# Gate times bias added to x by an accumulating DMA per group, in place of a product per tile on TensorE

## The reference, cut to what matters

```
mod = (silu(c) @ wmod).reshape(8, 6, 1, 512)
sa, ca, ga, sb, cb, gb = ...            # rows of each batch; ga and gb are gates
x = x + ga * attention(...)             # for most rows: x + ga * bo, the same row V for a whole batch
h = layernorm(x) * (1 + cb) + sb
xd = dequantised(quantise(h)); wd = dequantised(quantise(weight))
x = x + gb * (xd @ wd.T + bias)         # = x + xd @ (gb*wd).T + gb*bias
```

## Time and profile before

| | us |
|---|---|
| median of 3 runs (390.23 to 390.87) | 390.24 |
| profiled execution, its own time | 389.05 |
| its span | 387.2 |
| PE busy | 321.5 |
| DVE busy | 306.0 |
| ACT busy | 219.8 |
| POOL busy | 203.9 |
| mean granted TensorE clock | 0.942 |

### The profile page before, as it was taken

How to read it: one execution, slowest core, us unless ns; L and a number is a source line. 1 busy time by engine, 2 the same in 40 slices (tenths; PEclk the granted TensorE clock), 3 DMA queues, 4 the chain that set the end, 5 groups by cost and what they waited for, 6 DMA issues and landing times.

```text
span 387.2 us, 6242 instructions
## 1 busy us (share of the span) xinstructions
PE 321.5 (83%) x2302; PEld 244.5 (63%) x2302; DVE 306.0 (79%) x500; ACT 219.8 (57%) x498; POOL 203.9 (53%) x123
## 2 busy tenths in 40 slices
PE   2940075785999999999899998979999989985994
PEld 0100012574798887788787776868887777664883
DVE  1893497699864699698979787999887899799733
ACT  2001858573835777787594969677876776110310
POOL 2004886909928549554973868294939372600000
PEclk9995569589999999999999999999999999998999
DMA  7998445769945884959394869566955951102032
GB/s 264 387 407 318 95 70 212 124 215 298 200 156 124 260 148 179 186 197 216 112 239 158 203 163 246 137 172 164 268 123 182 210 139 69 42 0 109 25 139 81
DMA packets 23156, 68.10 MB, mean 176 GB/s; under 512 B 2563, under 2 KB 2692, under 8 KB 19022
## 3 DMA queue, kind: packets, MB, share of 16 engines
q1 hardware_dynamic: 14982, 51.67, 37.6%
q0 software_dynamic: 7392, 14.68, 23.9%
q10 hardware_dynamic: 752, 1.36, 1.2%
HBM read 50.50 MB, written 17.20 MB: 175 GB/s over the span
## 4 chain that ended last, share of the span: by engine, by line
PE 43%; DVE 28%; issue 9%; ACT 7%; POOL 6%; DMA 4%; SPq 1%; DVEq 0%; POOLq 0%; ACTq 0%
PE ps L574 8%; PE ps L575 8%; PE ps L579 8%; PE ps L557 4%; DVE DD L1002 3%; DVE XL L965 3%; PE ps L655 3%; DVE amax L984 3%; PE ps L531 2%; DVE WL L972 2%; PE ps L570 2%; DMA v_bc<-mod_scratch 2%; DVE X L1009 2%; POOL U L326 2%; POOL U L328 2%
## 5 line engine op out<-in xcount | busy, mean ns | idle before, releaser
L326 POOL TENSOR_TENSOR U<-U,c_bc 128x1024 f32<-128x1024 f32 x32 | 78.3, 2448 | 54.2 <-ACT U L391 54.2
L574 PE MATMUL ps<-WH,XH 128*128 128x512 f32 x256 | 101.7, 397 | 0.7 <-ACT XH L375 0.7
L575 PE MATMUL ps<-WL,XH 128*128 128x512 f32 x256 | 101.5, 396 | 0.0
L375 ACT ACTIVATE XH<-ps 128x512 fp32r<-128x512 f32 x64 | 37.9, 592 | 81.6 <-PE ps L557 81.5
L328 POOL TENSOR_TENSOR U<-U,sb_bc 128x1024 f32<-128x1024 f32 x32 | 76.8, 2400 | 2.5
L965 DVE TENSOR_TENSOR XL<-ps,XH 128x512 fp32r<-128x512 f32 x64 | 44.0, 687 | 39.8 <-ACT XH L375 39.7
L579 PE MATMUL ps<-WH,XL 128*128 128x512 f32 x256 | 69.7, 395 | 1.3 <-DVE XL L965 1.3
L391 ACT ACTIVATE U<-X,nmr,rstd 128x512 f32<-128x512 f32 x64 | 48.5, 808 | 27.9 <-DVE nmr L980 27.8
L579 PEld LDWEIGHTS ps<-WH,XL 128*128 128x128 f32 x256 | 48.5, 190 | 12.4 <-DVE XL L965 2.0
L575 PEld LDWEIGHTS ps<-WL,XH 128*128 128x128 f32 x256 | 48.8, 191 | 11.1
L402 ACT ACTIVATE unused<-X 128x512 bf16<-128x512 f32 x64 | 39.4, 618 | 28.5 <-POOL X L317 27.6
(11 more groups left out here) (209 smaller groups left out, 404.1 us busy)
## 6 DMA issues: line engine op xcount, KB each, us to landing
X<-in_x SPq DMA_DIRECT2D x16, 1024.0 KB, 4.9
out<-X SPq DMA_DIRECT2D x15, 1024.0 KB, 5.8
X<-mod_scratch POOLq DMA_DIRECT2D x14, 1024.0 KB, 10.1
X<-in_wmod SPq DMA_DIRECT2D x4, 1024.0 KB, 9.6
c_bc<-mod_scratch SPq DMA_DIRECT2D x6, 256.0 KB, 7.7
sb_bc<-mod_scratch SPq DMA_DIRECT2D x6, 256.0 KB, 7.8
Wd<-in_w SPq DMA_DIRECT2D x1, 1024.0 KB, 12.9
U<-in_wmod SPq DMA_DIRECT2D x1, 1024.0 KB, 15.0
```

The costliest lines, as they stand in the source:

```text
L326: nc.gpsimd.tensor_tensor(a, a, spread(c_bc[:, b % 2, :]), ALU.mult).then_inc(u_done, 1)
L574: M(bank, XH[:, n % 2, r], WH[:, b % 2, k, :], start=False, stop=False)
L575: M(bank, XH[:, n % 2, r], WL[:, b % 2, k, :], start=False, stop=False)
```

## The change

The product with G2 goes, and with it G2, its loads, its two rows in DRAM and the split of GBIAS. In their place POOL issues, behind modulate(g), an accumulating DMA of the row GBIAS into X1's slot of group g, of the same form as the one that adds V. `add_tile` waits for it at a group's first tile. Before the first one POOL waits until GBIAS is written to DRAM.

```
-            sp.wait_ge(g2_rows, 2)
-            sp.dma_start(mod_dram[:, GBH, :], XH[0:B, 0, :].bitcast(F32)).then_inc(g2_rows_out, 16)
-            sp.dma_start(mod_dram[:, GBL, :], XL[0:B, 0, :].bitcast(F32)).then_inc(g2_rows_out, 16)
-            sp.wait_ge(g2_rows_out, 32)
-            for b in range(2):
-                load_g2(b)
+            sp.wait_ge(gb_row, 1)
+            sp.dma_start(mod_dram[:, GBIAS, :], mrow[GBIAS]).then_inc(gbias_out, 16)
...
-                if t % 2 == 0 and 2 <= t and t + 2 < GROUPS:
-                    sp.wait_ge(y_done, TILES * t)
-                    load_g2((t + 2) // 2)
...
+            def add_row(g, which):
+                nc.gpsimd.dma_start(X1[:, g % XSLOTS, :, :],
+                                    mod_dram[g // 2:g // 2 + 1, which, :].unsqueeze(1).to_broadcast([P, TILES, D]),
+                                    accum_op=ALU.add).then_inc(x_added[g % XSLOTS], 16)
+
+
+            def add_bias(g):
+                if g == 0:
+                    pool.wait_ge(gbias_out, 16)
+                pool.wait_ge(z_done, TILES * (g + 1))
+                add_row(g, GBIAS)
...
                 modulate(g)
+                add_bias(g)
...
-                M(bank, onesr[:], G2[:, b % 2, :], start=True, stop=False)
                 pe.wait_ge(xh_done, n + 1)
                 for k in range(NC):
                     r = slice(k * P, (k + 1) * P)
-                    M(bank, XH[:, n % 2, r], WH[:, b % 2, k, :], start=False, stop=False)
+                    M(bank, XH[:, n % 2, r], WH[:, b % 2, k, :], start=k == 0, stop=False)
                     M(bank, XH[:, n % 2, r], WL[:, b % 2, k, :], start=False, stop=False)
...
-                W_.tensor_copy(XH[0:B, 0, :], mrow[GBIAS]).then_inc(g2_rows, 1)
-                dve.wait_ge(g2_rows, 1)
-                TT(XL[0:B, 0, :], mrow[GBIAS], XH[0:B, 0, :].bitcast(F32), ALU.subtract).then_inc(g2_rows, 1)
...
                 dve.wait_ge(y_done, n + 1)
+                if j == 0:
+                    dve.wait_ge(x_added[g % XSLOTS], 16 * additions(g, 1))
```

More of the change, by code:

```diff
@@ L24 @@
 XSLOTS = 6
-V, C, SB, GB, GBIAS, CA, SA, GA, GBH, GBL = range(10)
+V, C, SB, GB, GBIAS, CA, SA, GA = range(8)
 FIRST, LAST = -17, TILES * GROUPS
@@ L38, in build @@
 def build(nc, x, xh, WqT, WkT, WvT, WoT, bo, lna, BDs, rows, columns, masks, w, bias, cT, wmod, ident, out):
-    mod_dram = nc.dram_tensor("mod_scratch", (B, 10, D), F32, kind="Internal").ap()
+    mod_dram = nc.dram_tensor("mod_scratch", (B, 8, D), F32, kind="Internal").ap()
     xg = x.rearrange("b (g p j) d -> (b g) p j d", p=P, j=TILES)
@@ L59, in build @@
         Wd = sb("Wd", [P, NC, D])
-        G2 = sb("G2", [P, 2, D], F32R)
         onesr = sb("onesr", [P, P], F32R)
@@ L137, in build @@
         x_in = [sem(f"x_in{i}") for i in range(XSLOTS)]
-        x_summed = [sem(f"x_summed{i}") for i in range(XSLOTS)]
+        x_added = [sem(f"x_added{i}") for i in range(XSLOTS)]
         stored = [sem(f"stored{i}") for i in range(XSLOTS)]
@@ L142, in build @@
         sb_in = [sem(f"sb_in{i}") for i in range(2)]
-        g2_in = [sem(f"g2_in{i}") for i in range(2)]
         wmod_in = [sem(f"wmod_in{i}") for i in range(6)]
@@ L151, in build @@
          msp_in, msp2_in, head_stored, cleared, zeroed, dve_step, v_row_done, v_row_out, cs_rows_done,
-         cs_rows_out, g2_rows_out) = (sem(n) for n in (
+         cs_rows_out) = (sem(n) for n in (
              "c_loaded", "small_in", "vec_in", "w_in", "head_in", "xs_in", "lna_in", "bo_in", "wq_in", "wk_in", "wv_in",
              "wo_in", "scratch_out", "msp_in", "msp2_in", "head_stored", "cleared", "zeroed", "dve_step",
-             "v_row_done", "v_row_out", "cs_rows_done", "cs_rows_out", "g2_rows_out"))
-        (exp_c, silu_done, mod_mm, mod_cp, gb_row, g2_rows, rows2_done, gb_mm, gb_cp, wd_done, wscaled, wt_mm,
+             "v_row_done", "v_row_out", "cs_rows_done", "cs_rows_out"))
+        (exp_c, silu_done, mod_mm, mod_cp, gb_row, gbias_out, rows2_done, gb_mm, gb_cp, wd_done, wscaled, wt_mm,
          wt_high, wt_low, var_done, std_done, hs_done, hT_mm, hT_cp, q_mm, k_mm, v_mm, q_ready, kT_ready,
@@ L161, in build @@
          sxh_cp, sxl_done, sy_mm, head_out) = (sem(n) for n in (
-             "exp_c", "silu_done", "mod_mm", "mod_cp", "gb_row", "g2_rows", "rows2_done", "gb_mm", "gb_cp",
+             "exp_c", "silu_done", "mod_mm", "mod_cp", "gb_row", "gbias_out", "rows2_done", "gb_mm", "gb_cp",
              "wd_done", "wscaled", "wt_mm", "wt_high", "wt_low", "var_done", "std_done", "hs_done", "hT_mm",
@@ L180, in due, with additions @@
             return g if r == 0 and 0 <= g < GROUPS else None
+        def additions(g, bias):
+            return 2 * (g // XSLOTS) + (g % XSLOTS >= 2) + bias
         def mods(i):
@@ L192, in mod_row @@
                 sp.dma_start(buf, mod_dram[b:b + 1, which, :].to_broadcast([P, D])).then_inc(signal, 16)
-            def load_g2(b):
-                sp.dma_start(G2[0:2, b % 2, :].bitcast(F32), mod_dram[b, GBH:GBL + 1, :]).then_inc(g2_in[b % 2], 16)
             def chunked(a):
@@ L246, in _ @@
             sp.dma_start(mod_dram[:, GB, :], mrow[GB]).then_inc(scratch_out, 16)
-            sp.dma_start(mod_dram[:, GBIAS:GA + 1, :], late[0:B, :, :]).then_inc(scratch_out, 16)
+            sp.dma_start(mod_dram[:, CA:GA + 1, :], late[0:B, CA - GBIAS:, :]).then_inc(scratch_out, 16)
             sp.wait_ge(scratch_out, 32)
@@ L298, in _ @@
             nc.gpsimd.memset(LR[:].bitcast(F32), 0.0).then_inc(cleared, 1)
-            nc.gpsimd.memset(G2[:].bitcast(F32), 0.0).then_inc(cleared, 1)
             def spread(a):
                 return a.unsqueeze(1).to_broadcast([P, HALF, D])
+            def add_row(g, which):
[7 more added lines that the diff above has]
+                add_row(g, GBIAS)
             def add_attn_bias(g):
@@ L309, in add_attn_bias @@
                     pool.wait_ge(v_row_out, 16)
-                    nc.gpsimd.dma_start(X1[:, g % XSLOTS, :, :],
-                                        mod_dram[b:b + 1, V, :].unsqueeze(1).to_broadcast([P, TILES, D]),
-                                        accum_op=ALU.add).then_inc(x_summed[g % XSLOTS], 16)
+                    add_row(g, V)
                     return
@@ L369, in high_part @@
             def high_part(n):
-                if n == 0:
-                    act.wait_ge(g2_rows_out, 32)
                 if n >= 2:
@@ L397, in sums @@
                 else:
-                    act.wait_ge(x_summed[g % XSLOTS], 16 * (g // XSLOTS + (g % XSLOTS < 2 and -1 or 0) + 1))
+                    act.wait_ge(x_added[g % XSLOTS], 16 * additions(g, 0))
                 for j in range(HALF * h, HALF * (h + 1)):
@@ L564, in product @@
                     pe.wait_ge(wt_low, NC * (b + 1))
-                    pe.wait_ge(g2_in[b % 2], 16 * (b // 2 + 1))
-                if n == 0:
-                    pe.wait_ge(cleared, 4)
                 if n >= 2:
                     pe.wait_ge(o_done, n - 1)
-                M(bank, onesr[:], G2[:, b % 2, :], start=True, stop=False)
                 pe.wait_ge(xh_done, n + 1)
@@ L959, in low_part @@
             def low_part(n):
-                if n == 0:
-                    dve.wait_ge(g2_rows_out, 32)
                 if n >= 2:
```

## The result

The changed kernel takes 393.25 us (median of 20 runs, 389.81 to 398.17) against 390.26 us before (20 runs, 387.89 to 390.99): ratio 1.0074, 95% interval 1.0049 to 1.0098. It is slower, as forecast, but by 3 us and not by 10, and it scatters by 8 us where the kernel before scatters by 3. Medians here are over all executions of a kernel, while the ratios and their intervals leave out those more than 1.5% above its shortest. The profiled execution of the changed kernel took 395.31 us, 2 us above its median.

The account below looks back on a forecast made before the run. PE-led pipeline, DVE close behind; with the change, full DMA engines delay the last V: 12 us left less 2 us of PE saving, 10 us slower, 389.05 to 399, plus 1.2 for the median: 400 us; 8 in 10 range 383 to 416.

Parts of the forecast that it names:

- the place of the pressure: DMA engines: q0 at about twice its share, DMA share 0.9 or more from 60 to past 300 us, longer landings.
- The last V then lands at 319 and not at 294, 25 us late: End of the 60 to 294 us stretch: 254 us of DMA work, packed at 0.98, takes 259 us.
- step 47: Where ACT used the last V's data at 307.32 us: 13 us of slack, so 12 us left as delay.
- 6.4 us each: Time of all 16 DMA engines per accumulating DMA; 13 new ones ahead of the last V add 83 us.
- the density: Packing of the DMA engines from 60 us to the last V: 0.98 taken, between 0.91 and 1.05.
- PE's gain: 64 products removed from PE: 8.5 us, 2.2% of the chain, between 0 and 15 us.
- the forecast's mechanism: DMA engines' throughput over the steady part makes the last V late beyond ACT's slack: 10 us slower in sum, chance 0.54.
- only the start pays: Rival, chance 0.12: group 1's DMA delays x of group 4 at 80 to 100 us by 6 to 9; 387 to 393.
- some 0.4 us: Start: POOL first issues group 0's new DMA, so its scalings start this much later; start's DVE gain costed at 0.
- The DVE gain at the start: DVE loses the cast and the subtraction, 2.62 + 2.71 us; costed at 0, hidden by POOL and a load of x.
- TensorE's clock: Rival, chance 0.04: PE waits per group and its clock falls to 1.2 GHz each time, giving 405 to 415 us.
- The page's price: Trainium skill: 4.4 us per 1 MB DMA; by it 13 new DMAs take 31 us, fit idle time, kernel faster.

Follow-up runs that it names:

- Experiment 2: Changed kernel without the new DMAs of groups 0, 1 and 2 (their bias is missing): 388.5 us, ratio 0.9906 against the kernel before.
- experiment 11: Changed kernel with groups 0 and 1 by the product, the others by DMA, and 46 small matmuls at the start: 387.01 us, ratio 0.9918 against before.
- Experiment 8: Changed kernel with one more accumulating DMA of 0.75 MB behind each bias of groups 3 to 14: 429.61 us, ratio 1.1 against before.
- experiment 10: Changed kernel with only the new DMA of group 1 issued, the other groups' bias left out: 392.49 us, ratio 1.0068 against before.
- experiment 5: Changed kernel with no bias addition at all and 54 small matmuls in PE's idle time at the start: 383.13 us, ratio 0.9823 against before.
- experiments 5 and 6: The second of these: complete changed kernel with 54 small matmuls in PE's idle time at the start, 391.04 us, ratio 1.0031 against before.

## Why the prediction was right or wrong

**The sign** and the place of the pressure were right: q0 doubled, the share reached 0.99, loads went from 4.9 to 8.8 us and stores from 5.8 to 8.2, SP's wait for stores grew from 52.0 to 73.3 us, POOL's for x from 33.8 to 53.7, add_tile never waited for its new semaphore. One reading was too strong: the store of 271.44 us, of which the prediction says that it hardly moved, landed 6.3 us behind its issue, against a median of 5.8.

**The step that failed** is "The last V then lands at 319 and not at 294, 25 us late", and with it the 12 us that "are left as delay at step 47". The rows are the last V's issue, its size and time to landing in the changed kernel, the same before, and ACT's first use of that data in the changed kernel:

```profile
291.98 1.27 POOL L296 DMA_DIRECT2D X<-mod_scratch  x1 [0.87 <-DMA X<-in_x]
X<-mod_scratch POOLq DMA_DIRECT2D x1, 1024.0 KB, 17.7
X<-mod_scratch POOLq DMA_DIRECT2D x1, 1024.0 KB, 10.6
311.23 0.61 ACT L402 ACTIVATE unused<-X 128x512 bf16<-128x512 f32 x1
```

It landed at 309.7 us and before at 294.8: 15 us late and not 25. Two sizes were off. The new DMAs took less engine time than 6.4 us each: all queues together took 84.8% of 393.5 us, 334 us, and before 63.1% of 387.2, 244 us; so 90 us for 16, 5.6 each. In the stretch itself there were 0.99 x 249.7 = 247 us of work from 60 to 309.7 and not 254. And the density was 0.99, at the good side of the 0.98 that I took. ACT came to this data at 311.23 us, without a wait: the delay of 12 us at step 47 was nothing. A part of that is luck. Against ACT's time of before, 307.32, the data was 2 us late; it was in time because the start had already made everything 3.9 us later (the table at group 12). Experiment 2, which has no such delay and 10 of the 13 new DMAs ahead, still hides them: its last V landed at 297.6 us and ACT took it at 301.36. With 11 ahead, in experiment 11, ACT already waits 3.0 us in all. All 13 without the delay were not run.

What gave the 3 us was another sum: the start, put at nothing in the forecast, 7.4 us; the stop, 2.2 to 3.9 us; and PE's gain of 7.2 us against them, of which the forecast's sum counted 2. Experiment 8 fits the forecast's mechanism, with the reserve made there: 12 more DMAs of 0.75 MB cost 36 us.

**The rival "only the start pays"** was the one that happened: its place (x of group 4, behind group 1's DMA) and its price (6 to 9 us) came true with V of group 4 7.3 us late and 7.4 us in the medians, and the time, 393.25 us, lies just above its 387 to 393, with the stop in it that the rival doesn't have (391.04 without). In the mechanism it was half right, since it named group 1's DMA alone: that one gives 5.0 us of the 7.3 by itself. In experiment 10 it runs beside the load of x for 6.1 us and makes it 3.5 us longer: the load is slowed and not stopped. I had seen it and put it beside the sum, at 0.12, and not into it. Taking group 0's DMA at "some 0.4 us" was also short: POOL's side of it was right, but it holds the load of x for group 3, 3 us.

**PE's gain**, forecast 8.5 us: experiment 5 has 7.2 (390.3 to 383.1), so the chain's 2.2% was a good measure. But the change doesn't get it whole, for a reason that I didn't think of: removing the products moved a stop of PE into the densest row of its program. That took 3.9 us without the new DMAs (387.02 against 383.13) and 2.2 us with them (393.25 against 391.04). The DVE gain at the start, costed at 0, was 0: without any new DMA the first add_tile is at 81.7 and not at 81.9.

**TensorE's clock**, a rival at 0.04, fell where PE waited and not in every group: the mean granted clock is 0.80 from 60 to 110 us (0.86 before) and 0.99 from 110 to 294 us (1.00 before). No run parts what it cost from the waits ahead of it; it is within the prices above.

The ledger, from the medians: 390.3, less 7.2 for the products, plus 3.9 for the stop, plus 7.4 for the first three DMAs, less 1.2 (not told apart from nothing) for the other 13: 393.2. Each term is the difference of two neighbouring kernels, so that the sum has to come out; it is no test. By another way, over experiments 5 and 6, it reads 390.3 - 7.2 + 7.9 for all 16 DMAs + 2.2 for the stop: the single terms are known to 1 or 2 us.

**The page's price** of 4.4 us for a DMA of 1 MB from GpSimd, of which 2.4 move data (the Trainium skill, "DMA: Bandwidth & Descriptors", "Anatomy of one DMA"), stays wrong for accumulating ones: 12.5 us to landing, 5.6 of the engines. What I drew from it, that the steady part hides them, came true for another reason: 63 us of idle engine time, 13 of slack, and the delay of the start.

## What to carry to other kernels

A sum of engine time against a stretch decides only after the slack of whoever reads the data: compute both, and then look for the one place where there is no slack, here the start, where each late load is passed on whole. When a transfer can be chosen group by group, keep the old way where the queue is crowded (8 products of 0.24 us against 7 us of delay). And if instructions are removed from a dense stream, look for new stops with no releaser in the trace before judging the edit, and lay the packets of the queue "instruction" beside them.

## What the runs showed of the hardware that I had not expected

TensorE can stop for 2 to 5 us in the middle of a row of 32x32 matmuls with nothing to wait for but its own instructions. In eight kernels it was after exactly 111 of 128 (2.0, 2.15, 2.7, 3.5, 3.6, 3.8, 3.8 and, in the changed kernel, 4.7 us), with eight more products ahead after 106, and with 54, 46 or 38 small matmuls put ahead it was gone. In all nine a 16 KB packet of the queue "instruction" starts 2.4 to 3.1 us before PE goes on (table in experiment 5). The same holds for smaller stops at other places, in the changed kernel at 183 us (1.34 us, the packet 2.4 us before its end).

Not every wait that the profile calls "issue" is such a stop. One of 1.85 us, at 351.27 us in the changed kernel, stands in every kernel that has dropped all or most of the products; it ends when ACT has copied XH, which is late there because of the head's work on DVE, and the kernel before waits 1.44 us at the same place, put down to DVE:

```profile
350.71 0.58 ACT L375 ACTIVATE XH<-ps 128x512 fp32r<-128x512 f32 x1
351.27 0.47 PE L570 MATMUL ps<-WH,XH 128*128 128x512 f32 x1 [1.85 <-issue]
344.18 0.47 PE L570 MATMUL ps<-G,onesr 128*128 128x512 f32 x1 [1.44 <-DVE X L1009]
```

An accumulating DMA of 1 MB takes 6.4 us of the 16 engines in the kernel before. In the changed one the same count, by its queue's share, gives 6.1 us, and the growth of all queues' sum gives 5.6. Why is open.
